# A transformer block on one core: other first loads, batch 0 prepared by two engines, another order on every engine

## The reference

```
mod = (silu(c) @ wmod).reshape(16, 6, 1, 128)      # sa, ca, ga, sb, cb, gb
h = layernorm(x) * (1 + ca) + sa
q = softmax(h @ Wq.T + bq, within a head); k = softmax(h @ Wk.T + bk, over tokens); v = h @ Wv.T + bv
o = layernorm(q @ (k.T @ v), 128 channels) * ln_g + ln_b
x = x + ga * (o @ Wo.T + bo)
h = layernorm(x) * (1 + cb) + sb
p, e = top_k(softmax(h @ router_w), 2)
x = x + gb * sum over the 2 chosen e of p_e * (gelu(h @ w_in[e] + b_in[e]) @ w_out[e] + b_out[e])
```

## Time and profile before

| what | value |
|---|---|
| median of 3 runs | 372.89 us (371.85 to 373.71) |
| profiled execution | 372.75 us |
| its span, first to last instruction | 370.9 us |
| PE busy | 354.1 us, 95% of the span |
| PEld busy | 321.6 us, 87% |
| DVE busy | 291.2 us, 79% |
| ACT busy | 306.5 us, 83% |
| POOL busy | 226.5 us, 61% |

### The profile page before, as it was taken

The page is one execution under the profiler, slowest core; times in us unless marked ns, Lnnn a source line. Parts: engine busy times, 40 slices in busy tenths (PEclk is TensorE's granted clock), DMA queues, the critical chain, the costliest instruction groups (busy, mean ns, idle before and its releaser), DMA issues.

```text
span 370.9 us, 8258 instructions
## 1 busy us (share of the span) xinstructions
PE 354.1 (95%) x2532; PEld 321.6 (87%) x2532; DVE 291.2 (79%) x1063; ACT 306.5 (83%) x524; POOL 226.5 (61%) x220
## 2 busy tenths in 40 slices
PE   2987999999999999999999999999999999998996
PEld 1866879899999989999999989999999989997985
DVE  2799889987897967787897888888898978747653
ACT  3467899999999899899998999899977968885750
POOL 3255947595649666573838658494659856274551
PEclk9999999999999999999999999999999999999999
DMA  5155045352515262252707035350606051424481
GB/s 172 20 159 230 0 159 216 115 173 73 185 40 197 81 190 98 115 164 52 244 3 259 28 115 172 109 178 17 241 5 227 2 177 55 143 87 157 160 273 68
DMA packets 19106, 47.84 MB, mean 129 GB/s; under 512 B 2603, under 2 KB 6390, under 8 KB 18806
## 3 DMA queue, kind: packets, MB, share of 16 engines
q1 hardware_dynamic: 18432, 46.64, 37.7%
q10 hardware_dynamic: 630, 0.67, 0.6%
HBM read 42.82 MB, written 4.48 MB: 128 GB/s over the span
## 4 chain that ended last, share of the span: by engine, by line
PE 80%; DVE 7%; issue 6%; POOL 3%; ACT 2%; DMA 1%; ACTq 1%; DVEq 0%; POOLq 0%
PE pY L1052 27%; PE pH L1036 7%; PE pH L1038 7%; PE pH L1037 7%; PE pQV L1000 3%; PE pC L986 3%; PE pC L1007 3%; PE pB L1022 3%; PE pQV L978 2%; PE pQV L962 2%; PE pQV L964 2%; PE pQV L963 2%; PE pB L1014 2%; PE pA L941 2%; PE pC L994 2%
## 5 line engine op out<-in xcount | busy, mean ns | idle before, releaser
L1052 PE MATMUL pY<-wout,v 128*128 128x128 f32 x1024 | 130.7, 276 | 0.1
L1052 PEld LDWEIGHTS pY<-wout,v 128*128 128x128 f32 x1024 | 124.5, 192 | 4.6 <-DVE v L1516 0.8
L746 ACT ACTIVATE u<-pH,cols 128x512 f32<-128x512 f32 x128 | 85.3, 685 | 15.9 <-PE pH L1038 11.7
L427 POOL TENSOR_TENSOR v<-u,gate_bc 128x512 f32<-128x512 f32 x48 | 68.5, 1432 | 19.4 <-PE pY L1052 11.8
L1516 DVE TENSOR_TENSOR v<-u,gate_bc 128x512 f32<-128x512 f32 x80 | 62.0, 784 | 8.6 <-DMA gate_bc<-route_scratch 5.6
L1036 PE MATMUL pH<-h_hi,win_hi 128*128 128x512 f32 x128 | 59.0, 461 | 0.5 <-ACT u L746 0.5
L1037 PE MATMUL pH<-h_hi,win_lo 128*128 128x512 f32 x128 | 50.5, 395 | 0.0
L1038 PE MATMUL pH<-h_lo,win_hi 128*128 128x512 f32 x128 | 50.4, 394 | 0.0
L439 POOL TENSOR_TENSOR h_lo<-h,h_hi 128x512 fp32r<-128x512 f32 x16 | 20.3, 1272 | 36.0 <-ACT h_hi L674 36.0
L746 ACT ACT_TABLE_LOAD x27 | 34.6, 1283 | 0.5
L444 POOL TENSOR_TENSOR rstd<-ve,neg_half 128x4 f32<-128x4 f32 x16 | 18.7, 1168 | 23.9 <-DVE nm L1473 23.9
(11 more groups left out here) (156 smaller groups left out, 811.6 us busy)
## 6 DMA issues: line engine op xcount, KB each, us to landing
gate_bc<-route_scratch SPq DMA_DIRECT2D x64, 512.0 KB, 5.0
x_all<-in_L_attn_x SPq DMA_DIRECT2D x16, 256.0 KB, 5.0
out<-x_all SPq DMA_DIRECT2D x15, 256.0 KB, 2.6
gates<-gate_scratch SPq DMA_DIRECT2D x1, 1792.0 KB, 6.9
route_scratch<-gateT SPq DMA_DIRECT2D x64, 4.0 KB
gb_bc<-gb_scratch SPq DMA_DIRECT2D x1, 1024.0 KB, 7.9
win<-in_L_ffn_w_in SPq DMA_DIRECT2D x1, 512.0 KB, 5.6
wout<-in_L_ffn_w_out SPq DMA_DIRECT2D x1, 512.0 KB, 7.2
```

What stands on the lines that cost most here:

```text
L427: pool.tensor_tensor(v[:, e % U, :], u[:, e % U, :], gate_bc[:, b % 2, e, :], ALU.mult).then_inc(s["vp_done"], 1)
L746: act.activation(u[:, e % U, :], pH[:, e % 2, :], ACT.Gelu_apprx_tanh, bias=cols[:, e:e + 1]).then_inc(s["gelu_done"], 1)
L1052: i = mm(pY[:, t * P:(t + 1) * P], v[:, e % U, t * P:(t + 1) * P], wout[:, e, :], start=False, stop=(e == NE - 1), skip_group_check=True)
```

## The change

It does four things.

1. **Loads.** SP issues `wmod` right after x of batch 0, then all four attention weights, x1, the 16 pieces of `b_out`, x2, x3 and the bias rows. ACT issues `c`, computes silu, and then issues the four row loads and `bo`. The expert weights, which were issued after the first two batches' gates, are now issued after the gates of all other batches (1792 KB) and x of batch 4.
2. **Batch 0.** `ln1_apply(0)` does two of four tiles on ACT, `ln1_apply_first` the other two on DVE. `hT_first` turns two into `pA` and two into a free part of `pQV`; `h_evac_first` (ACT) and `h_evac_half` (DVE) scale and shift a half each, and `h_low_first` on DVE replaces POOL's `h_low(0)`. Counts of `xn1_ready` that later functions wait for are two lower.
3. **PE's first products.** Ten products of the identity stand around the transposition of silu; `modulation` goes ahead of the transposes of rows and weights; 8 of the 15 `keep_clock` are gone.
4. **Order.** The lists of all engines are another permutation of the same calls, under the same waits, from batch 0 to 15, and the repeating `step` of each engine is another.

```diff
             load_x(0)
-            for j, wt in ((0, Wq), (1, Wv)):
+            sp.dma_start(wmod_sb[:, :, :], wmod.rearrange("k (j c) -> k j c", j=NMOD)).then_inc(s["wmod_loaded"], DMA)
+            for j, wt in ((0, Wq), (1, Wv), (2, Wk), (3, Wo)):
                 sp.dma_start(w_nat[:, j, :], wt).then_inc(s["w_loaded"], DMA)
...
             act.dma_start(c_sb[:, :], c).then_inc(s["c_loaded"], DMA)
-            for j, wt in ((2, Wk), (3, Wo)):
-                act.dma_start(w_nat[:, j, :], wt).then_inc(s["w_loaded"], DMA)
-            act.dma_start(wmod_sb[:, :, :], wmod.rearrange("k (j c) -> k j c", j=NMOD)).then_inc(s["wmod_loaded"], DMA)
+            act.wait_ge(s["c_loaded"], DMA)
+            act.activation(silu_c[:, :], c_sb[:, :], ACT.Silu).then_inc(s["silu_ready"], 1)
...
+            def h_evac_first():
+                act.wait_ge(s["hT_done"], 1)
+                act.wait_ge(s["prep_mod"], 4)
+                half = slice(0, NTOK // 2)
+                act.activation(h_hi[:, half], pA[:, half], ACT.Identity, bias=modT[:, 0, 1:2], scale=modT[:, 0, 0:1])
+                act.activation(h[:, half], pA[:, half], ACT.Identity, bias=modT[:, 0, 1:2], scale=modT[:, 0, 0:1]).then_inc(s["hhi_ready"], 1)
...
+            pe.wait_ge(s["const_ready"], 1)
+            for _ in range(6):
+                mm(pH[:, 1, 0:P], ident[:, :], ident[:, :], start=True, stop=True)
+            pe.wait_ge(s["silu_ready"], 1)
+            pe.transpose(pH[:, 0, 0:NB], silu_c[:, :], ident[0:NB, 0:NB]).then_inc(s["tr_silu"], 1)
+            for _ in range(4):
+                mm(pH[:, 1, 0:P], ident[:, :], ident[:, :], start=True, stop=True)
...
+            def hT_first():
+                pe.wait_ge(s["xn1_ready"], T // 2)
+                for t in range(T // 2):
+                    pe.transpose(pA[:, t * P:(t + 1) * P], xn1[:, t, :], ident[:, :])
+                pe.wait_ge(s["xn1_half"], T // 2)
+                for t in range(T // 2, T):
+                    i = pe.transpose(pQV_flat[:, (t + 2) * P:(t + 3) * P], xn1[:, t, :], ident[:, :])
+                i.then_inc(s["hT_done"], 1)
...
+            def ln1_apply_first():
+                dve.wait_ge(s["nmr1_ready"], 1)
+                for t in range(T // 2, T):
+                    dve.tensor_scalar(xn1[:, t, :], x_all[:, 0, t, :], rstd1[:, t:t + 1], nmr1[:, t:t + 1], ALU.mult, ALU.add).then_inc(s["xn1_half"], 1)
...
+            def h_low_first():
+                dve.wait_ge(s["h_half"], 2)
+                dve.wait_ge(s["hhi_ready"], 1)
+                dve.tensor_tensor(h_lo[:, :], h[:, :], h_hi[:, :].bitcast(F32), ALU.subtract).then_inc(s["hlo_ready"], 1)
```

More of the change, by code:

```diff
@@ L1142, in _ @@
-            hidden(0, 4)
+            attend_project(2)
+            attend_centred(2)
+            logits(1)
+            qv(3)
             hidden(0, 5)
-            attend_centred(2)
-            h2T(1)
-            attend_project(2)
-            qv(3)
-            moe_bias(0)
-            logits(1)
+            hidden(0, 6)
             combine(0, 0)
-            hidden(0, 6)
+            ek_back(3)
             combine(0, 1)
+            combine(0, 2)
+            combine(0, 3)
+            gate_turn(1)
@@ L1238, in _ @@
[L1238 to L1248 removed]
+            hidden(3, 7)
+            ek_back(6)
+            gate_turn(4)
+            combine(3, 2)
+            combine(3, 3)
+            hidden(4, 0)
+            state(6)
+            hidden(4, 1)
@@ new lines, in _ @@
+            hT(7)
+            combine(3, 4)
+            combine(3, 5)
+            hidden(4, 2)
+            state_weights(6)
+            combine(3, 6)
+            combine(3, 7)
+            q_turn(6)
+            hidden(4, 3)
+            h2T(5)
+            hidden(4, 4)
+            kT(7)
+            attend_centred(6)
+            hidden(4, 5)
+            logits(5)
+            moe_bias(4)
+            qv(7)
+            hidden(4, 6)
+            combine(4, 0)
+            hidden(4, 7)
@@ L1617, in _ @@
             q_norm(1)
-            state_out(1)
-            ln1_stats(4)
+            expert_bias()
             k_max(2)
-            ln1_var(4)
             out_var(1)
             q_bias(2)
+            q_max(2)
+            route(0)
+            q_shift(2)
+            gates_out(0)
+            residual1(1)
+            ln2_stats(1)
             v_bias(2)
-            q_max(2)
+            ln2_var(1)
+            q_sum(2)
             k_inv(2)
-            q_shift(2)
-            route(0)
@@ L1629, in _ @@
-            residual1(1)
-            gates_out(0)
-            q_sum(2)
-            state_out(2)
-            ln2_stats(1)
-            q_inv(2)
-            ln2_var(1)
-            q_norm(2)
-            gates_turned(0)
-            expert_bias()
+            gates_turned(0)
+            q_inv(2)
+            q_norm(2)
+            state_out(2)
+            ln1_stats(4)
             k_max(3)
+            ln1_var(4)
+            weigh(0, 0)
+            weigh(0, 2)
+            route(1)
             out_var(2)
-            weigh(0, 0)
```

824 lines of the change are left out of this document (435 added, 389 removed).

## The result

The changed kernel takes 380.56 us (median of 4 executions, 378.88 to 381.89) where the kernel before, beside it, takes 372.97 (371.85 to 373.71): 1.020 times as long, 95% interval 1.017 to 1.023. The profiled execution took 379.39 us with a span of 377.7, against 372.75 and 370.9. The forecast was 370.1 with a range of 367.2 to 374.2: it was wrong in sign, and the time lies outside the range. Two of the four executions took 378.9 and 379.4, the other two 381.7 and 381.9; the trace is of the one of 379.39, so it holds 6.6 of the 7.6 us, and what the longer two lose on top no trace shows.

What follows compares the result with a forecast made beforehand. PE, busy nearly all of 57 to 320 us, was taken as the bound, leaving mainly the ends to win. From 372.75, minus 1.9 (start), 0.6 (middle) and 0.3 (end) gave 369.95, 370.1 for the median; range 367.2 to 374.2.

Steps and rivals of the forecast that it cites:

- Start up to kT(0): Loads and first products before kT(0): kT(0) at 11.4 to 12.1, 2.9 to 3.6 us ahead of 15.05.
- the 0.7 us put on it: Gain credited to the ten warm-up products raising PE's clock earlier; without it the sum would be 370.8.
- Batch 0: From kT(0) to kT(1): DVE gives most of the lead back, leaving 1.6 us at q_norm(0) and 1.85 at kT(1).
- Batches 1 to 3: Up to the first combine: moved DVE blocks hidden at first, then 1.1 us lost; lead 1.2, or 1.9 with earlier clock.
- the marker's set: Six hidden products of batch 0 and qv of batch 3, finished by the first combine at 56.98 us before.
- the 1.1 us for state(2): In batches 1 to 3, state(2) waits for v_bias(2) behind residual1(1) and ln2_stats(1), costing 1.1 us.
- The term: Lead up to the first combine: -1.9 us, with ends of -3.6 and +0.5.
- Rival 1: PE's clock falls again between qv(0) and hT(1), costing 2.5 us: 372.6, no change; chance 0.24.
- Middle: Repeating steps: nothing lost, and half of the 1.3 us over 20.97 a batch won back, -0.6 us.
- Rival 2: ACT's ring does not close, PE waits in about 11 batches; at 0.4 us over, +4.4 us, 375.1; chance 0.12.
- End: Last batches: the 0.7 us wait at gate_turn stays, attend_project(15) fills other waits; -0.3 us, between -1 and +1.

Runs made afterwards that it cites:

- e12b: Changed kernel's start up to about 33 us with seven added keep_clock products but no identity products, then all lists of the kernel before: 370.74 us, ratio 0.992.
- e8: The kernel before without 8 of its 15 keep_clock products: 374.21 us, ratio 1.006.
- e4: The changed kernel with 11 more keep_clock products: 375.89 us, ratio 1.008.
- f4: e12b with the bias loads right behind that of x1 and expert_gates behind state_out(0) on DVE: 372.15 us, ratio 0.999.
- e1: The changed start alone, with the lists of the kernel before behind kT(0) and qv(0): 377.47 us, ratio 1.009.

## Why the prediction was wrong, point by point

- **Start up to kT(0)** (11.4 to 12.1 forecast, 10.91 measured): right, 0.5 us too cautious. The clock was up well before 10, as said (the modulation's eight records took 0.96 us at 6.36; before, the same eight took 1.89 us), but the 0.7 us put on it had no effect at the end (e12b).
- **Batch 0** (q_norm(0) ending at 21.8, kT(1) at 22.75): 21.4 and 23.30. The mechanism was right, a DVE that never rests; what was missing is the low clock from 16.3 on.
- **Batches 1 to 3** (hidden(0, 0) at 41.0, the marker's set done at 55.8): 41.90, and about 58.9 (combine(0, 0), one hidden product later in the new order, started at 59.60). The step that failed is "at first this is hidden, as k_max(2) waits on a product anyway". expert_bias was priced at 2.6 us from the earlier trace rows, a row where POOL was out of its way, and took 4.7; and the 1.1 us for state(2) left out that hT(3) now waited for ek_evac(2), and this for q_shift(2) and exp_q(2). The term was -1.9 and is +1.8.
- **Rival 1** (the clock falls between qv(0) and hT(1), 2.5 us, chance 0.24) came true in its mechanism, and should have been in the sum: its evidence, the fall behind 367 in the earlier trace rows, was the better row. Its 2.5 us were too much. e8 prices one fall at 0.6 us at kT(1) and 1.5 us of span in all, e4 both falls at 1.4 us up to 60. The second fall, at 47, no rival had.
- **Middle** (-0.6, "each has a place"): +2.1. The step that failed is that the middle loses nothing. I went round ACT's ring and did not look at which DVE and POOL operations would stand side by side. The trace of before showed it in plain sight: the same form of operation with a mean far above its shortest. **Rival 2** had the right sign with the wrong mechanism; PE waited for DVE's qn, s2T and gate, not for ACT.
- **End** (-0.3): +2.8, the same mechanism at gates_out(14), gates_out(15), q_norm(15) and gates_turned(15). The step that failed is that only the one wait of 0.7 us at gate_turn stays: gate_turn(15) alone is now waited for 1.45 us. That attend_project(15) fills a wait is not seen, since other waits took its place.

## What to carry to other kernels

In an order for several engines, the price of an operation depends on what the engine beside it does at that moment, here on which of the two starts first; before trusting a new order, list the operations whose longest is far above their shortest and ask which of them PE reads next. Products that only keep the clock up are not waste while PE still waits: taking eight away from the kernel before cost 2.0 us (e8). A faster start is best joined to the old order whole: two or three single calls put back into the new one cost 3 to 5 us more, while start and old order together were 1.3 us (0.4%) and more faster than before.

## What the runs showed of the hardware

Over the traces a DVE operation with both inputs in SBUF (or a small tensor_scalar there, 0.17 us alone, 0.74 at 25.98 in f4, and once a cast) that starts behind a POOL operation over 128 columns or more ends after it: 0.02 to 0.15 us after when it is small (bout_rows at 35.73 ends 0.15 behind win_lo), 0.55 us after at 128x512 (197.25 + 1.29 = 198.54, q_norm ends at 199.09). POOL pays as well: its 128x512 operation took 1.74 in place of 1.27 us where it started during q_norm at 198.49. POOL's operations over 4 columns do not hold DVE up, long as they are, as here in the changed kernel:

```profile
211.17 1.00 POOL L431 TENSOR_TENSOR rstd_o<-ve_o,neg_half 128x4 f32<-128x4 f32 x1
211.78 0.69 DVE L1620 TENSOR_TENSOR v<-u,gate_bc 128x512 f32<-128x512 f32 x1 [0.39 <-PE pY L1113]
```

The granted clock fell to 0.50 at 16.34 in the changed kernel, where PE had been idle for 1.14 and 1.20 us with four transposes in between, and at 47.06, 1.9 us behind the end of an idle stretch of 2.31 us. In e1 it fell at 20.33, just behind an idle stretch of 4.79 us. In the kernel before the 1.20 us ahead of state(1) left it at 1.00.
